# Capacity-limited experts: a slot-to-token map, and gathers and scatters by slot tile

## The reference, cut to what matters

```
E, C, T = 128, 32, 8192
logits = xt @ wg                                # [T, E]
e1, e2 = the two largest;  g1, g2 = their softmax weights, divided by their sum
loc1 = number of earlier tokens whose first choice is e1
loc2 = the same for second choices, plus all first choices of that expert
v1, v2 = (loc1 < C), (loc2 < C)
buf[e * C + loc] += xt * v                      # [E*C, 128], 4096 slots
yb = einsum('ecd,edf->ecf', buf.reshape(E, C, d), we)
y = (g1 * v1) * yb[idx1] + (g2 * v2) * yb[idx2]
```

## Time and profile before

| what | value |
|---|---|
| runs | 6125.94, 6130.41, 6135.96 us; median 6130.41 |
| profiled execution, span from first to last instruction | 6118.5 us |
| its own device time | not listed apart; the runs shown are 7.4 to 17.5 us above the span |
| busy in the span | PE 5082.0 (83%), DVE 3494.7, ACT 3177.6, POOL 2473.6 us |
| changed phase | from 4106.0 to 4538.5 us of the span |
| granted TensorE clock, mean | 0.902 of full speed |

### The profile page before, as it was taken

One profiled execution on the slowest core, in us unless ns is written; L12 is line 12 of the kernel. 1 busy time (PEld: TensorE's weight loads), 2 busy tenths in 40 slices (PEclk: granted clock), 3 DMA queues, 4 the chain that ended last, 5 costly groups with the idle time before them and its releaser, 6 DMA issues. The chain is left out here.

```text
span 6118.5 us, 105868 instructions
## 1 busy us (share of the span) xinstructions
PE 5082.0 (83%) x38217; PEld 2622.6 (43%) x38217; DVE 3494.7 (57%) x5632; ACT 3177.6 (52%) x7160; POOL 2473.6 (40%) x2086
## 2 busy tenths in 40 slices
PE   6999789898977999997999999874237999974995
PEld 2444234344424666643566664442112222241784
DVE  5787422577845666643666654565338999730233
ACT  2666633366764666642566663342014888841552
POOL 3333000222216888831888871016562232116025
PEclk7999999799987999998999999886567999976997
DMA  3443111233410000020000000011112333211123
GB/s 102 111 119 111 41 45 50 64 103 107 115 32 20 8 7 6 5 82 19 8 6 6 7 3 4 2 42 27 36 35 68 90 90 97 59 46 49 52 78 91
DMA packets 329515, 312.95 MB, mean 51 GB/s; under 512 B 78758, under 2 KB 279106, under 8 KB 327106
## 3 DMA queue, kind: packets, MB, share of 16 engines
q1 hardware_dynamic: 312642, 285.77, 16.4%
q0 software_dynamic: 16384, 20.69, 1.3%
HBM read 172.15 MB, written 136.32 MB: 50 GB/s over the span
## 5 line engine op out<-in xcount | busy, mean ns | idle before, releaser
L806 ACT ACTIVATE a_prob<-a_PB 128x512 f32<-128x512 f32 x2304 | 1253.1, 597 | 453.0 <-PE a_PB L648 337.5
L696 PE MATMUL a_PO<-a_prob,a_V 128*32 128x256 f32 (+3 forms) x8192 | 713.3, 421 | 22.6 <-ACT a_cn L779 22.3
L960 DVE TENSOR_REDUCE a_blocks<-a_PA 128x8 f32<-128x1024 f32 x512 | 602.1, 1215 | 37.6 <-PE a_PA L648 35.1
L963 DVE TENSOR_REDUCE a_neg<-a_PA 128x2 f32<-128x1024 f32 x512 | 591.0, 1213 | 34.5 <-PE a_PA L661 34.5
L661 PE MATMUL a_PA<-a_KS,a_QS 48*128 48x512 bf16 (+3 forms) x3072 | 470.4, 345 | 109.7 <-DVE a_blocks L960 68.5
L2534 DVE TENSOR_REDUCE f1a_neg<-f1a_PA 128x2 f32<-128x384 f32 (+1 forms) x512 | 267.1, 522 | 489.1 <-PE f1a_PA L2336 488.6
L2464 POOL TENSOR_TENSOR f1a_prob<-f1a_prob,f1a_inv 128x384 f32<-128x384 f32 (+1 forms) x512 | 395.3, 775 | 283.4 <-DVE f1a_inv L2538 283.4
L678 PE MATMUL a_PB<-a_QS,a_KS 51*128 51x512 bf16 (+3 forms) x3072 | 447.7, 329 | 57.2 <-ACT a_prob L806 55.3
L2428 ACT ACTIVATE f1a_pt<-f1a_PT 128x512 f32<-128x512 f32 (+1 forms) x512 | 278.8, 544 | 348.5 <-PE f1a_PT L2345 344.8
L2421 ACT ACTIVATE f1a_prob<-f1a_PA,f1a_neg 128x192 f32<-128x192 f32 (+1 forms) x1024 | 406.2, 405 | 68.0 <-DVE f1a_neg L2534 67.9
L661 PEld LDWEIGHTS a_PA<-a_KS,a_QS 48*128 48x128 bf16 x3072 | 123.6, 94 | 632.8 <-DVE a_blocks L960 200.3
(11 more groups left out here) (422 smaller groups left out, 10380.5 us busy)
## 6 DMA issues: line engine op xcount, KB each, us to landing
a_spill<-a_qkp SPq DMA_DIRECT2D x96, 384.0 KB
a_QS<-a_spill SPq DMA_DIRECT2D x384, 96.0 KB, 2.5
a_KS<-a_spill SPq DMA_DIRECT2D x384, 96.0 KB, 2.5
a_spill<-a_qkp SPq DMA_DIRECT2D x96, 256.0 KB
a_raw<-a_cn SPq DMA_DIRECT2D x192, 72.0 KB
a_spill<-a_qkp SPq DMA_DIRECT2D x96, 128.0 KB
f_rows<-tokens_in SPq DMA_DIRECT2D x78, 128.0 KB
tokens_out<-f_rows SPq DMA_DIRECT2D x78, 128.0 KB
```

Of the source, the lines that this page charges most:

```text
L696: mm = nc.tensor.matmul(PO[32 * j:32 * j + 32, first:last], V[:, par, t, 8 * e + pr], prob[:, k % st.ring, e, c + first - q0:c + last - q0 ...
L806: nc.scalar.activation(prob[:, k % st.ring, e], PB[:, ring_b.slot(0, ("b", s, e))], ACT.Exp, scale=scale).then_inc(pb_used, 1)
L960: nc.vector.tensor_reduce(to, of, AX, ALU.max).then_inc(pa_used, 1)
L963: nc.vector.tensor_reduce(neg[:, t, pr], PA[:, bank:bank + 2], AX, ALU.max, negate=True).then_inc(pa_used, 1)
```

## The change

The two DRAM tensors get other contents. `token_rows` (4 MB) holds every token's row, stored by SP in 16 direct DMAs. `choice_rows` (8 MB) holds one row for each token and choice. The kernel builds the reverse map, from slot to token. The triangle gets 2^15 (`OWN`) on its diagonal, so that a maximum along the experts gives a token's own place plus 2^15, without the product with M. VectorE compares this with the 32 place numbers (`seat`, a one-hot of the place), GpSimd multiplies this by the token's two code numbers, its lane and its tile plus 64 for a second choice plus 1 (`who`), and TensorE multiplies M by `who`, summing all 32 groups in one PSUM bank: expert by place, the code of the token that sits there. Eight small products regroup this into 32 slot tiles, four experts in each, and VectorE makes source and target addresses. Then, for each slot tile, GpSimd gathers 128 token rows, TensorE transposes and multiplies, and GpSimd scatters 128 result rows into choice_rows. Six gathers run ahead; xin has 8 buffers, y has 4. The sum then reads choice_rows by 16 direct DMAs of SP (512 KB each, both choices), ScalarE weighs the first choice and VectorE the second, and rows of dropped choices are read as the zeros that the earlier phase has put there: choice_rows is cleared in place of slots_in.

```diff
+OWN = 1 << 15
-    XG = E128 // 16
-    CP = TT // 2
+    XT = E128 // 4
+    AHEAD = 6
...
-        M = sb("M", [P, 3, 4, E128], BF16)
+        M = sb("M", [P, 4, 4, E128], BF16)
...
 SP:
-            sp.wait_ge(scattered, 16 * 2 * TT)
-            (8 loads of slots_in, 8 stores to slots_out)
+            for g in range(NG):
+                sp.wait_ge(rowed, g + 1)
+                sp.dma_start(token_rows[:, 4 * g:4 * g + 4], rows[:, 4 * g:4 * g + 4]).then_inc(kept, 16)
+            for r in range(4):
+                sp.wait_ge(sent[r], 16 * (XT // 4))
+            for b in range(B):
+                if b >= 4:
+                    sp.wait_ge(mixed, b - 3)
+                sp.dma_start(got_rows[:, b % 4], choice_rows[:, :, 4 * b:4 * b + 4]).then_inc(fetched[b % 4], 16)
 TensorE:
+            def name_seats(k):
+                pe.wait_ge(coded, k + 1)
+                for j in range(4):
+                    mm = nc.tensor.matmul(PI[:, 0:2 * CAP], M[:, k % 4, j], who[:, k % 2, j].rearrange("p a n -> p (a n)"),
+                                          start=(k == 0 and j == 0), stop=(k == 2 * NG - 1 and j == 3))
+                mm.then_inc(mapped, 1)
...
             for k in range(NG, 2 * NG):
                 rank(k)
+                name_seats(k - 1)
+            name_seats(2 * NG - 1)
...
 ScalarE:
-            for k in range(XG):
+            for k in range(XT):
                 act.wait_ge(product, k + 1)
-                if k >= 2:
-                    act.wait_ge(stored[k % 2], 16 * (k // 2))
+                if k >= 4:
+                    act.wait_ge(sent[k % 4], 16 * (k // 4))
...
 GpSimd:
-            (128 scatters to slots_in, 128 gathers of slots_out)
+            for k in range(2 * NG):
+                pool.wait_ge(seated, k + 1)
+                if k >= 2:
+                    pool.wait_ge(mapped, k - 1)
+                nc.gpsimd.tensor_tensor(who[:, k % 2], seat[...], code[...], ALU.mult).then_inc(coded, 1)
+            pool.wait_ge(kept, 16 * NG)
+            pool.wait_ge(addressed, 2)
+            for k in range(AHEAD):
+                gather(k)
+            for k in range(XT):
+                if k + AHEAD < XT:
+                    gather(k + AHEAD)
+                send(k)
 VectorE, place(k):
-                nc.vector.tensor_tensor(own[:], PR[...], M[:, k % 3], ALU.mult).then_inc(used, 1)
-                (sum over the experts, then four small linked operations)
+                nc.vector.tensor_reduce(k4, PR[...], AX, ALU.max).then_inc(used, 1)
+                dve.wait_ge(used, k + 1)
+                if k >= 2:
+                    dve.wait_ge(coded, k - 1)
+                nc.vector.tensor_tensor(seat[:, k % 2], place_iota[...], k4[...], ALU.is_equal).then_inc(seated, 1)
...
 glu_phase:
-                for buf in (net.buf, net.xbuf):
+                for buf in (net.ybuf, net.xbuf):
```

More of the change, by code:

```diff
@@ L1413, in slot_experts_phase @@
         den = sb("den", [P, TT])
[L1414 to L1418, removed]
+        loc = sb("loc", [P, 2 * TT])
+        seat = sb("seat", [P, 2, 4, CAP], BF16)
+        who = sb("who", [P, 2, 4, 2, CAP], BF16)
+        held = sb("held", [P, 2, CAP], BF16)
+        lo, hi = sb("lo", [P, XT]), sb("hi", [P, XT])
+        second, empty = sb("second", [P, XT]), sb("empty", [P, XT])
+        source, target = sb("source", [P, XT], U32), sb("target", [P, XT], U32)
         PL = psum("PL", [P, 2, S])
@@ L1422, in slot_experts_phase @@
         PB = psum("PB", [P, S])
[L1424 to L1428, removed]
+        PI = psum("PI", [P, S])
+        xin = rows[:, 0:8]
+        xT = rows[:, 8:10]
+        y = rows[:, 10:14]
@@ L1441, in slot_experts_phase @@
+        fetched = [sem(f"fetched{r}") for r in range(4)]
+        first_weighed, mixed, c_turned, x_added = sem("first_weighed"), sem("mixed"), sem("c_turned"), sem("x_added")
         block = ctx.enter_context(nc.Block())
@@ L1498, in rank @@
                 mm.then_inc(ranks, 1)
+                if k == 2 * NG - 1:
+                    return
                 if k:
@@ L1586, in _ @@
+            act.wait_ge(weights, 1)
+            for b in range(B):
+                act.wait_ge(fetched[b % 4], 16 * (b // 4 + 1))
+                for t in range(4):
+                    n = 4 * b + t
+                    ins = nc.scalar.activation(got_rows[:, b % 4, 0, t], got_rows[:, b % 4, 0, t], ACT.Copy, scale=tot[:, n:n + 1])
+                ins.then_inc(first_weighed, 1)
         @block.gpsimd
         def _(pool):
[L1588 to L1607, removed]
+            pool.wait_ge(consts, 2)
@@ new lines, in send @@
+            def send(k):
+                pool.wait_ge(y_out, k + 1)
+                nc.gpsimd.indirect_dma_start(
+                    out=net.ybuf, out_offset=bass.IndirectOffsetOnAxis(ap=target[:, k:k + 1], axis=0),
+                    in_=y[:, k % 4], in_offset=None, bounds_check=2 * TT * P - 1, oob_is_err=False).then_inc(sent[k % 4], 16)
+            pool.wait_ge(kept, 16 * NG)
+            pool.wait_ge(addressed, 2)
+            for k in range(AHEAD):
+                gather(k)
+            for k in range(XT):
+                if k + AHEAD < XT:
+                    gather(k + AHEAD)
+                send(k)
@@ L1673, in _ @@
             link(nc.vector.reciprocal(den[:], den[:]))
[L1674 to L1681 removed]
+            nc.vector.tensor_tensor(g2[:], g2[:], den[:], ALU.mult)
+            nc.vector.tensor_tensor(tot[:], tot[:], den[:], ALU.mult).then_inc(weights, 1)
+            for k in range(XT):
                 dve.wait_ge(x_turned, k + 1)
```

183 lines of the change are left out of this document (96 added, 87 removed).

## The result

The changed kernel took 0.9659 of the time before, 95% interval 0.9643 to 0.9675: 209 us less, where 189.5 were forecast. The runs before had a median of 6131.48 us; those after took 5909.3, 5919.24 and 5935.17 us (a fourth, 10335.38 us at a clock of 0.49, is left out). Two further comparisons gave 0.9676 (0.966 to 0.9692) and 0.9687 (0.9669 to 0.9705), so the change is worth 190 to 210 us. The profiled execution is the one of 5935.17 us.

What follows compares the result with a forecast made beforehand. GpSimd's queue of scatters and gathers was taken to bound the phase. Routing 114, experts 91 and sum 38 us make 243 in place of 432.5: 189.5 us off 6130.4 gives 5941 us, range 5920 to 5992.

Steps and rivals of the forecast that it cites:

- stage A: Routing up to the first gather: 114 us (105 to 150) against 219 before with the scatters.
- stage B: Experts with 32 gathers and 32 sends on GpSimd's queue: 91 us (84 to 120) against 33 before.
- Group period 3.9 us: Routing, first choices: VectorE sets the pace, its period per group falling from 5.08 to 3.9 us.
- Second choices at 2.1 us: Routing, second choices: period per group 2.1 us, between 1.6 and 2.5, against 2.75 before; 34 us in all.
- Long hand-offs: Very late hand-offs between engines end with the scatters; 2 us allowed in routing, upper end 35 us.
- Contention: GpSimd's new product and VectorE hinder each other in routing: 3 us allowed, ends 0 and 21.
- Tail 5 us: End of routing, from the last reduction through regrouping and VectorE's small operations: about 5 us.
- Rival 1: Long hand-offs stay in routing (33 us) and experts (20 us) beyond the allowances: 5994 us; chance 0.15.
- Rival 2: Four result tiles set the expert stage, sends landing after 13.8 us: 42 us more, 5983 us; chance 0.08.
- Rival 3: One engine crossing of 15.23 us in each expert step: 486 us more, 6427 us; chance 0.02.
- Stage C: Weighted sum from 16 direct loads, VectorE the limit: 38 us (34 to 55) against 180.5 before.
- The fill: Larger zero fill in the earlier phase: hidden under 94 us of cover; 19 us without it.

Runs made afterwards that it cites:

- e2: Kernel before the change without the 64 scatters of the second choices: 6061.11 against 6119.91 us, ratio 0.9909.
- e3: Changed kernel with its 32 sends replaced by direct stores of SP, so GpSimd issues only gathers: 5889.0 us, ratio 0.9613 to before.
- e4: Changed kernel with its 32 gathers replaced by direct loads of SP, so GpSimd issues only sends: 5884.86 us, ratio 0.9603 to before.
- e7: Changed kernel with the product with the mask put back before the maximum on VectorE: 5945.45 us, ratio 0.9724 to before.
- e5: Changed kernel with the token-coding product (who) made by VectorE instead of GpSimd: 5932.24 us, ratio 0.9699 to before.
- e6: Changed kernel with a ring of two result tiles instead of four: 5914.47 us, ratio 0.9667 to before.
- e1: Kernel before the change with 6 MB more to clear in the earlier phase: 6122.53 against 6119.91 us, ratio 1.0.
- e8: Changed kernel with ten gathers ahead instead of six, 12 input and 8 result buffers: 5923.97 us, ratio 0.967 to before.
- e9: Changed kernel with the experts' tiles taken in pairs, half the signals and copies, eight result tiles: 5914.65 us, ratio 0.9664 to before.
- e10: e9 with both masks made by comparing logits in the first pass, without the index search: 5904.87 us, ratio 0.966 to before.

## Why the prediction was right, step by step

- **What bounds the phase** (GpSimd's queue, 339 us of it removed): right. e2 takes half of the scatters away, and 64 x 1.28 = 82 us of queue gave 57.6 of time, since VectorE then set the pace. e3 and e4 show it for the stage after. The phase gained 201 us, 11.4 more than forecast; the errors of stage A and stage B are of opposite sign, so the sum is nearer than its terms.
- **Group period 3.9 us**: right, 3.90. e7 and e5 show that VectorE sets it. The 2 us added for the first groups at 1.2 GHz did not come: the first pass ended 67.9 us into the phase (4179.43), where 70 were forecast.
- **Second choices at 2.1 us, taken between 1.6 and 2.5**: too high. The choice rested on TensorE at 1.2 GHz; it was granted 2.4 there, and VectorE's 1.62 us set the pace. 16 x 0.48 = 7.7 us by the periods (27.1 us from 4179.43 to the last reduction at 4206.53, where 34 were put), the largest error of the sum. The lower bound had been worked out; the clock at which the stage would run was not.
- **Long hand-offs, 2 us allowed in stage A**: there were none. The longest idle time of ScalarE in the second pass before its last copy is 1.72 us, and stage A issues no indirect DMA. e2 shows this to be the right reason.
- **Contention, 3 us allowed (0 to 21)**: none on the path. The product did become 0.39 us longer beside the mask, in GpSimd's slack. The rule of the Trainium skill, SBUF — State Buffer (SBUF: two separate sides), gives the shared ports to whichever of the two instructions starts first, for its whole length, and lets the other wait. The trace agrees in this: the mask began first in all 16 pairs, kept its 0.69 us, and the product became 0.39 us longer, somewhat less than the 0.53 us in which they overlapped. What the prediction left out was the order. It let the compare and the mask wait for a whole product, but neither ever began inside one, so the 21 us did not come, and no run here tests that case.
- **Tail 5 us**: 4211.89 - 4206.53 = 5.4 from the last reduction to the first gather. So the 13.6 us by which stage A was too long are 2.3 of the first pass, 6.7 of the second and 5 of allowances that were not needed, less 0.4 of the tail.
- **Stage B, 83 + 3.5 + 4**: 84.5 + 1.3 + 9.5 were measured. The queue took 1.33 us each, not 1.30. The 3.5 us for the last send's landing came from a misread row: the line under slots_in in the earlier trace rows is that of 2 fills and 8 direct loads (2.7/3.1/3.6 us by themselves), and no row there has a scatter's landing. A send had landed 2.3 us after its issue, 1.3 after its end. The idle time was 9.5 in place of 4. Rival 1 was half true: its hand-offs stayed in stage B, at 5.5 us beyond the allowance and not 20, and at nothing in stage A. My argument against it, that no such wait stood in the gather stage of before, was weak, for there TensorE hands over once in four gathers and is not waited for (0.4 us in all); e3 finds late hand-offs beside gathers too.
- **Rival 2**: a send had landed 2.3 us after its issue, not 13.8, so the ring never set the step; e6 halves the ring at no cost. The argument against it was a wrong one: the 13.8 us of the earlier trace rows are not those of scatters with a shared count. With its window on the zero fill alone (2720 to 2800) the view of tokens_in gives the same 8.1/13.8/20.6, so they are the ten direct fills of up to 1 MB each.
- **Rival 3**: no crossing of 15.2 us in the stage, and nothing near 5.9 us a step: 95.3 / 32 = 3.0 us a step.
- **Stage C, 38 us**: 35.9, with the limit where it was put. **The fill, hidden**: right, shown by e1.

What stays open is the mechanism by which TensorE's signals come late. Shown is that they do so only beside indirect DMAs of GpSimd (e2, and stage A against stage B), that each time GpSimd's queue ran dry both waiting engines went on soon after, and that neither deeper rings (e8) nor half as many signals (e9) cure it. The Trainium skill, Runtime: NRT & Kernel Launch (Instruction fetch mechanics), calls fetch mostly hidden. The trace agrees: over stage B its DMA view lists two packets for each of the two instruction queues, too few for the nine late copies of VectorE and nine of ScalarE.

## What to carry to other kernels

When a queue of small indirect DMAs sets the time, count them: a map computed on idle TensorE columns that turns 256 into 64 was worth 200 us here, and each DMA that goes is worth 1.2 to 1.3 us until another engine sets the pace. After such a change ask at once which engine sets the pace next and take work from that one (e5, e7 and e10 moved the end by what VectorE gained or lost). Price a stage at both levels of TensorE's clock, not only at the one that the old stage was granted, and see which engine sets the pace at each. Before a landing time is used, narrow the view to the DMAs that are meant: here the landing line of a tensor was that of other DMAs, and two forecasts rested on it.

## What the runs showed of the hardware

- Beside indirect DMAs issued back to back, work that TensorE had finished was taken up by VectorE or ScalarE up to 9.6 us late, with gathers and sends in turn. In e2 the late one came through 2.5 us after the last DMA's end. In the changed kernel GpSimd ran dry at 4234.27, and ScalarE and VectorE went on at 4236.35 and 4236.41; twice more it was 2.5 and 1.6 us from the end of GpSimd's DMA to ScalarE's copy (4263.68 to 4266.22, 4294.52 to 4296.10).
- A 128x256 product on GpSimd took 0.61 us by itself and 1.00 us beside a 128x512 compare of VectorE with two inputs in on-chip memory that had begun 0.16 us before it. The compare stayed at 0.69 us. Beside MAX8 the product kept its 0.61 us.
- A send of 128 rows of 512 bytes had landed 2.3 us after its issue: 2.34 and 2.38 us to the copy that waits for it in e6, 2.27 to 2.29 us from the last send to the load that waits for it in the profiles of the changed kernel and of e4 to e10.
